# One normalisation moves from VectorE to ScalarE in each of 16 units, and the second copy of the head outputs is made by an SBUF-to-SBUF transfer

## The chip, the cores and the metric

The kernel runs on 1 core of one Trainium2 chip. The metric is the device time of one launch in microseconds (us), and the median of several runs is compared. The core has four compute engines that run their own instruction lists in order: TensorE (PE in the rows; PEld is its weight load), VectorE (DVE), ScalarE (ACT) and GpSimd (POOL). SyncE (SP) only issues transfers here. The lists meet at semaphores.

## The reference

One layer of each kind is applied to a tensor of 4 sequences, 512 tokens, 256 features: attention, feed-forward, a state-space layer, feed-forward again. The change touches the attention alone:

```python
q_c = _rms_norm(x @ wq_down.T, q_norm_w)
kv_c = _rms_norm(x @ wkv_down.T, kv_norm_w)          # 64 wide, shared by the 16 heads
...
scores = jnp.einsum('bqhd,bkhd->bhqk', q, k) * scale
scores = jnp.where(causal[None, None], scores, -jnp.inf)
probs = jax.nn.softmax(scores.astype(jnp.float32), axis=-1)
out = jnp.einsum('bhqk,bkhd->bqhd', probs, v)
return out.reshape(bs, seq_len, NH * D_V) @ wo.T
```

## The kernel before

**Number format.** Nearly every product is made in split precision: a float32 tile is copied out of PSUM in a rounded format (the "hi" part, ScalarE), and VectorE writes the remainder ("lo"). The compressed values are only 64 wide, so the head outputs are kept as 64 rows of hi and 64 rows of lo in PSUM.

**Tiling.** Attention works on 4 batches. A batch has 4 tiles of 128 query tokens, a tile 4 groups of 4 heads, so a batch has 16 units; unit `n` belongs to tile `n // 4`. Because of the causal mask a unit of tile t has scores of width (t + 1) x 128 and t + 1 blocks of transposed probabilities. The last tile (units 12 to 15 of a batch) is the widest: 512 columns a head.

**Order.** Each engine's order is written out by hand as a slot function (`pe_slot`, `act_slot`, `dve_slot`), called once for each slot `s`. In one slot the engines work on several units at once: scores and row maxima of unit s-2 and s-3, exponentials of s-3, normalisation of s-3 and s-4, transposes of s-4, values of s-5, projection of s-6. Batches follow each other without a gap. Some slots carry extra work for the next batch (down projection, squares, feature-major copies).

**Steps that the change touches.**

- `exp` (L872) writes unnormalised probabilities of one head and their sum; `recip` (L1217, DVE) turns the sums of two heads into reciprocals. `normalise` multiplies one head's probabilities by its reciprocal: on ScalarE at L897, on VectorE at L1232. `on_dve` (L51) says which: before the change, heads 2 and 3 of a unit of the last tile go to VectorE, all others to ScalarE.
- `p_transpose(b, n, j)` (L1609, PE, matmuls at L1619) needs all four heads of unit n. In `pe_slot` it follows `q_transpose` (L1593).
- `pt_high` (L906, ACT) and `pt_low` (L1241, DVE) copy the transposed block; `values` (L1633 and L1636, PE) multiplies it by the values.
- `out_high` (ACT) copies the finished 4 head outputs of a unit out of PSUM bank 6 twice: at L912 all 128 rows into `o_a`, at L914 the 64 hi rows again into the upper half of `o_b`. `out_low` (L1247, DVE) writes the remainder of the hi rows into the lower half of `o_b`.
- `project(b, n)` (L1639, PE, matmuls at L1646 and L1648) multiplies `o_a` and `o_b` by the output weights. It stands one slot after `out_high` of the same unit. `o_a`, `o_b` have two buffers, by `n % 2`.
- SyncE's list (L722) has, after the loads of the weights, four loads for the state-space weights (`ssm_nat`), and then the stores of the output.

Of the kernel before, what the change touches and what calls it, by code (L numbers as in the profile page):

```python
# [4 lines left out]
F32 = mybir.dt.float32  # L5
# [14 lines left out]
G = 4  # L20
# [19 lines left out]
def tile_of(n):  # L40
    return n // (HEADS // G)
# [8 lines left out]

def on_dve(n, h):  # L51

    return tile_of(n % UNITS) == TB - 1 and h >= 2


def by_dve(n, k=0):
# [6 lines left out]
def by_act(n, k=0):  # L63
    return G * n + k - by_dve(n, k)
# [16 lines left out]
def token_count(b, k):  # L81

    return 1 + 14 * b + k - 4 * (b - (k == 0)) if b else 1 + k


def free_after(e, sem, count):

    if not (isinstance(count, int) and count <= 0):
        e.wait_ge(sem, count)
# [18 lines left out]
def build(nc, x_in, wq_down, wq_up, wq_rope, q_norm_w, wkv_down, kv_norm_w, wkv_up, wk_rope, wo,  # L108
# [3 lines left out]
    with ctx:  # L112
# [121 lines left out]
        def sem(name):  # L234
            return ctx.enter_context(nc.semaphore(name))
# [29 lines left out]
        recip_s, norm_a, norm_d = sem("recip_s"), sem("norm_a"), sem("norm_d")  # L265
        pt_mm, pt_hi_s, pt_lo_s, pv_mm = sem("pt_mm"), sem("pt_hi_s"), sem("pt_lo_s"), sem("pv_mm")
        o_hi_s, o_lo_s, y_mm = sem("o_hi_s"), sem("o_lo_s"), sem("y_mm")
        x_add, f_add, s_add = sem("x_add"), sem("f_add"), sem("s_add")

        gu_mm, silu_s, hf_s, hhi_s, hlo_s, dn_mm = (  # L270
# [452 lines left out]
        def _(sp_):  # L723
# [31 lines left out]
                sp_.wait_ge(prep_act, V0 + 4 * k + 4)  # L755
                sp_.dma_start(wo_b[KR:P, hs, :].bitcast(F32), wo_a[KR:P, hs, :].bitcast(F32)).then_inc(wo_b_in, 16)

            sp_.wait_ge(tok, token_count(BATCH, 0))
            sp_.wait_ge(at_mm, 1 + 3 * BATCH)
            sp_.dma_start(ssm_nat[:, 0, :, :], w_in.rearrange("(c p) d -> p c d", p=P)).then_inc(ssm_in, 16)  # L760
            sp_.dma_start(ssm_nat[:, 2, :, :], w_out.rearrange("(c p) d -> p c d", p=P)).then_inc(ssm_in, 16)
            hpc = P // (DIM // 32)
            for c in range(CK):
                sp_.dma_start(ssm_nat[:, 1, c, :],
                              w_dt[c * hpc:(c + 1) * hpc, :].unsqueeze(1).to_broadcast([hpc, DIM // 32, DIM]))\
                    .then_inc(ssm_in, 16)
            for b in range(BATCH):
                for t in range(TB):
                    sp_.wait_ge(f_add, BATCH * TB + b * TB + t + 1)
# [51 lines left out]
        def _(act):  # L821
# [87 lines left out]
            def out_high(b, n):  # L909
                act.wait_ge(pv_mm, b * BLOCKS + blocks_before(n + 1))  # L910
                free_after(act, y_mm, b * UNITS + n - 1)
                nc.scalar.copy(o_a[:, n % 2, :, :].rearrange("p h d -> p (h d)"), bank[6][:, :])\  # L912
                    .then_inc(o_hi_s, 1)
                nc.scalar.copy(o_b[0:KR, n % 2, :, :].rearrange("p h d -> p (h d)"), bank[6][0:KR, :])\  # L914
                    .then_inc(o_hi_s, 1)


# [206 lines left out]
        def _(dve):  # L1124
# [92 lines left out]
            def recip(b, n, k):  # L1217

                dve.wait_ge(s_exp, 1 + b * HEADS * TB + G * n + 2 * k + 2)
                if on_dve(n - 2, 2 * k):  # L1220
                    free_after(dve, norm_d, b * by_dve(UNITS) + by_dve(n - 2, 2 * k + 2))
                else:
                    free_after(dve, norm_a, b * by_act(UNITS) + by_act(n - 2, 2 * k + 2))
                nc.vector.reciprocal(rden[:, n % 2, 2 * k:2 * k + 2], den[:, n % 2, 2 * k:2 * k + 2])\  # L1224
                    .then_inc(recip_s, 1)

# [16 lines left out]
                    .then_inc(pt_lo_s, 1)  # L1243

            def out_low(b, n):
                dve.wait_ge(o_hi_s, 2 * (b * UNITS + n) + 2)
                nc.vector.tensor_tensor(o_b[KR:P, n % 2, :, :].rearrange("p h d -> p (h d)"), bank[6][0:KR, :],  # L1247
                                        o_a[0:KR, n % 2, :, :].rearrange("p h d -> p (h d)"), ALU.subtract)\
                    .then_inc(o_lo_s, 1)
# [299 lines left out]
        def _(pe):  # L1549
# [88 lines left out]

            def project(b, n):  # L1639
                g = n % (HEADS // G)  # L1640
                pe.wait_ge(o_hi_s, 2 * (b * UNITS + n) + 2)
                pe.wait_ge(o_lo_s, 1 + b * UNITS + n + 1)
                if g == 0:
                    pe.wait_ge(x_add, 1 + b * TB + tile_of(n))
# [266 lines left out]
```

## Time and profile before

| quantity | us |
|---|---|
| median of 3 runs | 808.61 |
| lowest and highest of them | 807.47, 811.57 |
| the profiled execution | 804.74 |
| its span, first to last instruction | 802.9 |

The page of the profile gives busy time by engine, the chain of work that ended last, and groups of instructions. The attention lasts from about 30 to 551 us of the span, the other layers from there on. In the attention all four engines are busy most of the time, so a share of busy time decides little; the chain of work, read in order of time, shows which engine's work each stretch waits for. Where two records on one engine follow each other without idle time, the second starts before the first one's record ends, so the cost of an instruction in a full queue is the distance between starts and not the length of its record.

### The profile page before, as it was taken

How to read it: one execution, taken by the hardware profiler on the slowest of the kernel's cores; microseconds unless marked ns; L12 is line 12 of the kernel's file. 1: busy time of each engine (PE TensorE's matmuls, PEld its weight loads, DVE VectorE, ACT ScalarE, POOL GpSimd, SP SyncE). 2: the span in 40 equal slices, each digit the busy share in tenths (PEclk: the TensorE clock that was granted, in tenths of full speed). 3: DMA queues.
4: the chain of work that ended last, by engine and by line, in shares of the span. 5: the costliest groups of instructions: out<-in, count | busy, mean ns of one | idle time of the engine just before them, and what ended most of it. 6: DMA issues, size and time to landing. Idle time of an engine off the chain costs nothing.

```text
span 802.9 us, 15139 instructions
## 1 busy us (share of the span) xinstructions
PE 749.6 (93%) x4556; PEld 645.8 (80%) x4556; DVE 668.8 (83%) x2184; ACT 603.3 (75%) x1499; POOL 468.2 (58%) x392
## 2 busy tenths in 40 slices
PE   4889999999999999999999999989999999999998
PEld 4768788888878788888887888777888788887887
DVE  4978998998999998899998999987676878877643
ACT  3459999888999988999887899985447576674232
POOL 0579999999999999999999999950000000000000
PEclk9899999999999999999999999999999999999999
DMA  9821000000000000000001000000000000000000
GB/s 228 266 67 28 2 1 1 1 1 2 1 2 2 1 1 2 1 2 1 1 2 41 1 2 1 1 1 1 1 1 1 0 1 1 1 17 11 27 27 27
DMA packets 15536, 15.58 MB, mean 19 GB/s; under 512 B 5824, under 2 KB 14464, under 8 KB 15072
## 3 DMA queue, kind: packets, MB, share of 16 engines
q1 hardware_dynamic: 13952, 12.45, 5.5%
q0 software_dynamic: 624, 2.12, 0.8%
q8 instruction: 38, 0.62, 0.3%
q14 instruction: 42, 0.34, 0.1%
q10 hardware_dynamic: 880, 0.04, 0.1%
HBM read 11.46 MB, written 2.10 MB: 17 GB/s over the span
## 4 chain that ended last, share of the span: by engine, by line
PE 60%; ACT 14%; DVE 10%; issue 9%; DVEq 0%; ACTq 0%
PE bank L671 12%; PE bank L673 11%; PE bank L672 11%; PE bank L1619 7%; ACT prob L897 5%; ACT prob L877 3%; PE bank L1633 2%; PE bank L1636 2%; PE bank L1646 2%; DVE pt_lo L1241 2%; PE bank L1648 2%; ACT pt_hi L906 2%; PE bank L636 1%; DVE o_b L1247 1%; PE bank L1582 1%
## 5 line engine op out<-in xcount | busy, mean ns | idle before, releaser
L810 POOL TENSOR_SCALAR hot<-raw_gu,lut 128x352 f32<-128x352 int32 x120 | 177.4, 1478 | 12.2
L816 POOL TENSOR_TENSOR total<-total,hot 128x352 f32<-128x352 f32 (+1 forms) x168 | 160.3, 954 | 14.0
L877 ACT ACTIVATE prob<-bank,bias_m 128x128 f32<-128x128 f32 (+3 forms) x256 | 136.2, 532 | 19.5 <-DVE bias_m L1189 19.0
L1189 DVE CUSTOM_DVE_ANT_0 bank<-bank,mask 128x128 f32<-128x128 f32 (+3 forms) x256 | 125.7, 494 | 21.1 <-issue 19.4
L1241 DVE TENSOR_TENSOR pt_lo<-bank,pt_hi 128x512 fp32r<-128x512 f32 x160 | 109.0, 682 | 8.2 <-ACT pt_hi L906 7.3
L1619 PE MATMUL bank<-ident,prob 128*128 128x128 f32 x640 | 99.3, 278 | 17.0 <-ACT prob L897 10.0
L897 ACT ACTIVATE prob<-prob,rden 128x128 f32<-128x128 f32 (+3 forms) x224 | 110.6, 545 | 4.5 <-DVE rden L1224 3.9
L906 ACT CAST pt_hi<-bank 128x512 fp32r<-128x512 f32 x160 | 94.2, 589 | 13.2 <-PE bank L1636 7.2
L1619 PEld LDWEIGHTS bank<-ident,prob 128*128 128x128 f32 x640 | 72.9, 140 | 35.5 <-ACT prob L897 19.3
L810 POOL TENSOR_SCALAR hot<-raw_dn,lut 128x352 f32<-128x352 int32 (+1 forms) x60 | 87.6, 1459 | 6.1
L671 PE MATMUL bank<-kt_hi,qt_hi 128*128 128x128 f32 (+3 forms) x256 | 87.2, 341 | 1.8 <-ACT prob L877 1.3
L673 PE MATMUL bank<-kt_hi,qt_lo 128*128 128x128 f32 (+3 forms) x256 | 82.6, 322 | 0.0
L672 PE MATMUL bank<-kt_lo,qt_hi 128*128 128x128 f32 (+3 forms) x256 | 82.5, 322 | 0.0
L671 PE MATMUL bank<-xt_hi,gu_hi 128*128 128x512 f32 (+1 forms) x176 | 70.1, 399 | 1.6 <-DVE h_f L1391 1.6
L1633 PE MATMUL bank<-pt_hi,v_hl 128*128 128x512 f32 x160 | 68.1, 426 | 2.6 <-issue 2.4
L673 PE MATMUL bank<-xt_hi,gu_lo 128*128 128x512 f32 (+1 forms) x176 | 69.4, 394 | 0.0
L672 PE MATMUL bank<-xt_lo,gu_hi 128*128 128x512 f32 (+1 forms) x176 | 69.3, 394 | 0.0
L1646 PE MATMUL bank<-wo_a,o_a 128*128 128x256 f32 x256 | 67.9, 298 | 0.1
L992 ACT ACTIVATE silu<-bank 128x512 f32<-128x512 f32 x40 | 23.9, 597 | 56.7 <-PE bank L673 56.7
L1648 PE MATMUL bank<-wo_b,o_b 128*128 128x256 f32 x256 | 63.7, 282 | 0.0
L1636 PE MATMUL bank<-pt_lo,v_hl 128*128 128x512 f32 x160 | 63.3, 396 | 0.3 <-DVE pt_lo L1241 0.2
L671 PEld LDWEIGHTS bank<-kt_hi,qt_hi 128*128 128x128 f32 x256 | 48.5, 189 | 11.8 <-issue 2.4
(214 smaller groups left out, 2084.0 us busy)
## 6 DMA issues: line engine op xcount, KB each, us to landing
x<-in_L_attn_a_x_dram SPq DMA_DIRECT2D x4, 512.0 KB, 7.8
wo_nat<-in_L_attn_a_wo_dram SPq DMA_DIRECT2D x1, 2048.0 KB, 14.6
out_dram<-x SPq DMA_DIRECT2D x16, 128.0 KB, 1.8
wqu<-in_L_attn_a_wq_up_dram SPq DMA_DIRECT2D x2, 768.0 KB, 8.5
wo_b<-wo_a SPq DMA_DIRECT2D x2, 512.0 KB, 4.3
wqr<-in_L_attn_a_wq_rope_dram SPq DMA_DIRECT2D x4, 192.0 KB, 7.0
raw_dn<-in_L_ffn_down_idx_dram POOLq DMA_DIRECT2D x1, 688.0 KB, 7.8
raw_gu<-in_L_ffn_gate_idx_dram POOLq DMA_DIRECT2D x1, 640.0 KB, 5.2
```

What stands on the lines that cost most here:

```text
L671: nc.tensor.matmul(o, l_hi, r_hi, start=start and k == 0, stop=False)
L672: nc.tensor.matmul(o, l_hi, r_lo, start=False, stop=False)
L673: last = nc.tensor.matmul(o, l_lo, r_hi, start=False, stop=stop and k == n - 1)
L810: nc.gpsimd.tensor_scalar((hot if v else total)[:, 0:n], raw[:, c:c + n], float(v), lut[:, v:v + 1], ALU.is_equal, ALU.mult).then_inc(lut_ ...
L816: nc.gpsimd.tensor_tensor(dst, total[:, 0:n], hot[:, 0:n], ALU.add).then_inc(lut_sum, 1)
L877: nc.scalar.activation(prob[:, n % 2, h, 0:w], bank[2 + h % 2][:, 0:w], ACT.Exp, bias=bias_m[:, n % 2, h:h + 1], scale=-1.0, accum_out=den ...
L897: nc.scalar.activation(prob[:, n % 2, h, 0:w], prob[:, n % 2, h, 0:w], ACT.Copy, scale=rden[:, n % 2, h:h + 1]).then_inc(norm_a, 1)
L906: nc.scalar.copy(pt_hi[:, c % 2, :, :].rearrange("p h d -> p (h d)"), bank[4 + c % 2][:, :])\
L1189: nc.vector.tensor_tensor_reduce(out=bank[2 + h % 2][:, 0:w], in0=bank[2 + h % 2][:, 0:w], in1=mask[:, TB * P - w:TB * P], scale=1.0, scal ...
L1241: nc.vector.tensor_tensor(pt_lo[:, c % 2, :, :].rearrange("p h d -> p (h d)"), bank[4 + c % 2][:, :], pt_hi[:, c % 2, :, :].rearrange("p h ...
L1619: last = nc.tensor.transpose(bank[4 + c % 2][:, h * P:(h + 1) * P], prob[:, n % 2, h, j * P:(j + 1) * P], ident[:, :])
L1633: nc.tensor.matmul(bank[6][:, :], v, pt_hi[:, c % 2, :, :].rearrange("p h d -> p (h d)"), start=j == 0, stop=False)
```

## The change

In the last tile VectorE normalises head 3 alone, and ScalarE heads 0, 1 and 2. ScalarE's second copy in `out_high` is gone; SyncE waits for the first copy of each unit and issues a transfer of its upper 64 rows, 128 KB, from `o_a` to `o_b`, which raises one of two new semaphores, `o_dup`. `project` waits for it as well. `out_low` waits for one copy instead of two. The four `ssm_nat` loads move in SyncE's list behind the transfer of the first unit of the last batch, 49 transfers in. `recip` waits for ScalarE's normalisation of two units before in all cases, and for VectorE's where head 3 is among them.

```diff
 def on_dve(n, h):
-    return tile_of(n % UNITS) == TB - 1 and h >= 2
+    return tile_of(n % UNITS) == TB - 1 and h == G - 1
...
+            def duplicate(b, n):
+
+                sp_.wait_ge(o_hi_s, b * UNITS + n + 1)
+                sp_.dma_start(o_b[0:KR, n % 2, :, :].bitcast(F32), o_a[0:KR, n % 2, :, :].bitcast(F32)).then_inc(o_dup[n % 2], 16)
+
+            for b in range(BATCH):
+                for n in range(UNITS):
+                    duplicate(b, n)
+                    if b == BATCH - 1 and n == 0:
+                        load_ssm()
...
                 nc.scalar.copy(o_a[:, n % 2, :, :].rearrange("p h d -> p (h d)"), bank[6][:, :])\
                     .then_inc(o_hi_s, 1)
-                nc.scalar.copy(o_b[0:KR, n % 2, :, :].rearrange("p h d -> p (h d)"), bank[6][0:KR, :])\
-                    .then_inc(o_hi_s, 1)
...
-                if on_dve(n - 2, 2 * k):
+                free_after(dve, norm_a, b * by_act(UNITS) + by_act(n - 2, 2 * k + 2))
+                if on_dve(n - 2, 2 * k + 1):
                     free_after(dve, norm_d, b * by_dve(UNITS) + by_dve(n - 2, 2 * k + 2))
-                else:
-                    free_after(dve, norm_a, b * by_act(UNITS) + by_act(n - 2, 2 * k + 2))
...
-                dve.wait_ge(o_hi_s, 2 * (b * UNITS + n) + 2)
+                dve.wait_ge(o_hi_s, b * UNITS + n + 1)
...
-                pe.wait_ge(o_hi_s, 2 * (b * UNITS + n) + 2)
+                pe.wait_ge(o_hi_s, b * UNITS + n + 1)
+                pe.wait_ge(o_dup[n % 2], 16 * ((b * UNITS + n) // 2 + 1))
```

ScalarE, two slots of the last tile in the second batch, before. L897 is a normalisation, L877 an exponential, L912 and L914 the two copies of head outputs:

```order
426 L912 CAST o_a<-bank 128x512
427 L914 CAST o_b<-bank 64x512
428 L877 ACTIVATE prob,den<-bank,bias_m 128x512
429 L906 CAST pt_hi<-bank 128x512
430 L877 ACTIVATE prob,den<-bank,bias_m 128x512
431 L884 COPY q_tok<-bank 128x4x64
432 L897 ACTIVATE prob<-prob,rden 128x512 x2
433 L906 CAST pt_hi<-bank 128x512
434 L877 ACTIVATE prob,den<-bank,bias_m 128x512
435 L906 CAST pt_hi<-bank 128x512
```

and the same stretch of the changed kernel, whose lines are 13 higher on this engine (L925 is the copy, L910 the normalisation):

```order
404 L925 CAST o_a<-bank 128x512
405 L890 ACTIVATE prob,den<-bank,bias_m 128x512
406 L919 CAST pt_hi<-bank 128x512
407 L890 ACTIVATE prob,den<-bank,bias_m 128x512
408 L897 COPY q_tok<-bank 128x4x64
409 L910 ACTIVATE prob<-prob,rden 128x512 x2
410 L919 CAST pt_hi<-bank 128x512
411 L910 ACTIVATE prob<-prob,rden 128x512
412 L890 ACTIVATE prob,den<-bank,bias_m 128x512
413 L919 CAST pt_hi<-bank 128x512
```

The copy into `o_b` has gone behind L925, and the third normalisation stands behind the copy of a transposed block and ahead of the next unit's first exponential.

VectorE at the same place, before, with what each instruction waits for:

```order
785 L1189 ISA bias_m 128x1
786 L1232 TENSOR_SCALAR prob<-prob,rden 128x512 [waits recip_s] x2
787 L1241 TENSOR_TENSOR pt_lo<-bank,pt_hi 128x512 [waits pv_mm,pt_hi_s]
788 L530 MEMSET scratch 128x1 [waits s_exp,s_mm]
789 L1189 ISA bank,bias_m<-bank,mask 128x512
```

and of the changed kernel:

```order
785 L1200 ISA bias_m 128x1
786 L1242 TENSOR_SCALAR prob<-prob,rden 128x512 [waits recip_s]
787 L1251 TENSOR_TENSOR pt_lo<-bank,pt_hi 128x512 [waits pv_mm,pt_hi_s]
788 L531 MEMSET scratch 128x1 [waits s_exp,s_mm]
789 L1200 ISA bank,bias_m<-bank,mask 128x512
```

One of the two normalisations ahead of the remainder copy is gone; the rest stands as it stood.

## Rows read from the trace of the kernel before

**Rows 1.** The page: busy time, its share of the span, and instructions by engine

```profile
PE 749.6 (93%) x4556; PEld 645.8 (80%) x4556; DVE 668.8 (83%) x2184; ACT 603.3 (75%) x1499; POOL 468.2 (58%) x392
```

**Rows 2.** Windows of the second batch: start:end, length, then busy us of each engine

```profile
205.00:232.00 27.00, 25.58 (x169) 22.15 (x169) 25.84 (x106) 26.70 (x84) 25.05 (x22) 1.00 0.01 2
...
262.00:297.00 35.00, 33.72 (x198) 28.18 (x197) 33.94 (x100) 30.61 (x70) 32.60 (x27) 1.00 0.00 1
```

**Rows 3.** Chain that ended last, in time: start, us, what; all around head-output copies

```profile
69.33 0.45 ACT o_b L914
...
212.72 0.45 ACT o_b L914
213.17 0.37 ACT squares L856 x2
...
542.70 0.48 ACT o_b L914
```

**Rows 4.** The same chain around one transposition of tile 2, and of the last tile

```profile
245.41 0.24 PE bank L1636
...
246.22 1.13 ACT prob L897 x2
...
247.39 0.66 PE bank L1619 x4
...
290.15 0.24 PE bank L1636
...
290.55 0.69 DVE pt_lo L1241
...
291.37 0.63 PE bank L1619 x4
...
514.92 0.48 DVE prob L1232
```

**Rows 5.** ScalarE's instructions in order of time: start, us, line, op, tiles

```profile
258.13 0.60 ACT L914 CAST o_b<-bank 64x512 fp32r<-64x512 f32 x1
258.61 0.60 ACT L877 ACTIVATE prob<-bank,bias_m 128x384 f32<-128x384 f32 x1
...
269.80 1.35 ACT L897 ACTIVATE prob<-prob,rden 128x512 f32<-128x512 f32 x2
271.04 0.59 ACT L906 CAST pt_hi<-bank 128x512 fp32r<-128x512 f32 x1
...
280.54 0.71 ACT L877 ACTIVATE prob<-bank,bias_m 128x512 f32<-128x512 f32 x1
```

**Rows 6.** VectorE's pairs of normalisations in three slots of the last tile

```profile
271.09 1.69 DVE L1232 TENSOR_SCALAR prob<-prob,rden 128x512 f32<-128x512 f32 x2
...
280.07 0.89 DVE L1232 TENSOR_SCALAR prob<-prob,rden 128x512 f32<-128x512 f32 x2
```

**Rows 7.** TensorE between the query transposes and the transposes of probabilities, two slots

```profile
271.88 0.60 PE L1593 MATMUL bank<-ident,q_tok 128*128 128x128 f32 x4
272.88 0.63 PE L1619 MATMUL bank<-ident,prob 128*128 128x128 f32 x4 [0.41 <-issue]
...
281.75 0.60 PE L1619 MATMUL bank<-ident,prob 128*128 128x128 f32 x4
```

**Rows 8.** Last units: ScalarE's first copy, and the first matmul of the projection

```profile
542.11 0.59 ACT L912 CAST o_a<-bank 128x512 fp32r<-128x512 f32 x1
547.78 0.58 ACT L912 CAST o_a<-bank 128x512 fp32r<-128x512 f32 x1 [1.32 <-PE bank L1636]
...
547.58 0.28 PE L1646 MATMUL bank<-wo_a,o_a 128*128 128x256 f32 x1
...
549.71 0.36 PE L1646 MATMUL bank<-wo_a,o_a 128*128 128x256 f32 x1
```

**Rows 9.** Transfers, from the page: count, KB each, median us from issue to landing

```profile
out_dram<-x SPq DMA_DIRECT2D x16, 128.0 KB, 1.8
...
wo_b<-wo_a SPq DMA_DIRECT2D x2, 512.0 KB, 4.3
```

More of the change, by code:

```diff
@@ L267, in build @@
         o_hi_s, o_lo_s, y_mm = sem("o_hi_s"), sem("o_lo_s"), sem("y_mm")
+        o_dup = [sem(f"o_dup{k}") for k in range(2)]
         x_add, f_add, s_add = sem("x_add"), sem("f_add"), sem("s_add")
@@ L756, in _, with load_ssm @@
                 sp_.dma_start(wo_b[KR:P, hs, :].bitcast(F32), wo_a[KR:P, hs, :].bitcast(F32)).then_inc(wo_b_in, 16)
[L758 to L766, printed above, removed]
+            def load_ssm():
+                sp_.wait_ge(tok, token_count(BATCH, 0))
+                sp_.wait_ge(at_mm, 1 + 3 * BATCH)
+                sp_.dma_start(ssm_nat[:, 0, :, :], w_in.rearrange("(c p) d -> p c d", p=P)).then_inc(ssm_in, 16)
+                sp_.dma_start(ssm_nat[:, 2, :, :], w_out.rearrange("(c p) d -> p c d", p=P)).then_inc(ssm_in, 16)
+                hpc = P // (DIM // 32)
+                for c in range(CK):
+                    sp_.dma_start(ssm_nat[:, 1, c, :],
+                                  w_dt[c * hpc:(c + 1) * hpc, :].unsqueeze(1).to_broadcast([hpc, DIM // 32, DIM]))\
+                        .then_inc(ssm_in, 16)
+            def duplicate(b, n):
[6 more added lines that the diff above has]
+                        load_ssm()
             for b in range(BATCH):
```

## The prediction, made before the changed kernel ran

> **What bounds the kernel now.** I read the totals first: TensorE is busy for 93% of the span, VectorE 83%, ScalarE 75% [rows 1]. That says the four lists are close together, not which one a given slot waits for. So I went to the windows of one attention batch [rows 2]. In a stretch of tiles 1 and 2 (205 to 232 us) ScalarE is busy 26.70 of 27.00 us, more than TensorE's 25.58. In the last tile (262 to 297) ScalarE falls to 30.61 of 35.00, and TensorE (33.72) and VectorE (33.94) are the full ones. The change takes work from ScalarE in every unit and gives it some in the last tile, which is where it has room.
>
> Busy time is still only a rate. What an edit can gain is read in the chain of work that ended last, since taking work off it shortens the program by that much at most, and work beside it gives nothing. The second copy L914 stands on that chain 15 times out of 64 (first at 69.33, last at 542.70 us), once with 0.00 us and otherwise with about 0.45 to 0.58 us each, 6.6 us in all [rows 3]. Where it does, the piece behind it is ScalarE's too (213.17, the squares): ScalarE runs without a gap and everybody waits for it. The other 49 are elsewhere. In tile 2 the chain is TensorE back to back, then two normalisations (246.22, 1.13 us), then the transposes at 247.39; the copy had been done before [rows 4]. In the last tile it goes from the values at 290.15 over the remainder copy on VectorE (290.55, 0.69 us) to the transposes at 291.37, a loop between TensorE and VectorE that holds neither the copy nor a normalisation [rows 4].
>
> **The second copy, removed.** In a full queue it costs the distance between starts: from 258.13 to 258.61, 0.48 us, not the 0.60 of its record [rows 5]. The 64 of them are 30.7 us of ScalarE's time, and the 49 off the chain are worth nothing by it. On the chain 6.6 us is the ceiling. Another path can stand close behind, and then less comes back: I take 6.0 us and keep 3.3 (half) and 6.6 as ends. I choose near the ceiling because in these slots TensorE has room of its own: its busy time in the window is 1.42 us short of 27.00, and busy time counts the overlap of pipelined matmuls, so the true room is larger. One of the 15 also releases `out_low`, which now starts after the first copy; that is the entry at 542.70 and is in the sum.
>
> **One normalisation of two, taken from VectorE (16 units).** A pair takes 0.89 us in one unit and 1.69 us in another [rows 6], so a single one costs VectorE 0.4 to 0.9 us. Mostly that frees nothing, by the loop above: the remainder copy behind the pair waits for TensorE anyway. The exception is the first unit of each last tile. There the query transposes start at 271.88 and the transposes of probabilities at 272.88, 1.00 us later [rows 7], while another slot of the same tile has the second group directly behind the first; the pair, at 271.09 with 1.69 us, ends at 272.78 and sets the start. Only in the last batch has the printed chain such a piece (514.92, 0.48 us [rows 4]). I take 0.4 us in each of 4 batches, 1.6 us; the ends are 0 (ScalarE's third normalisation is then what TensorE waits for) and 3.6 (0.9 us each).
>
> **The third normalisation, added on ScalarE.** It costs the distance between starts, half of 271.04 minus 269.80, 0.62 us, so 9.9 us over 16 units [rows 5]. Against the 0.48 us given back in the same slot ScalarE is 0.14 us longer in a slot where it has over 1 us idle (4.39 us of 35.00 in four slots [rows 2]), so its rate costs nothing. Its place could: TensorE waits for it before the transposes. In the slot at 280 us it would start where the exponential starts now (280.54) and end 0.73 us later (1.35 for two, less the 0.62 between their starts), at 281.3; the transposes start at 281.75 [rows 5, 7]. It is hidden with 0.45 us to spare. Queued behind it are the next exponential, a copy of a transposed block and the query copy, each later by 0.62 us; ScalarE's idle time takes that up. In the tail, after the last unit's queries, there is nothing to overlap and TensorE waits closely for each copy: 0.3 us there, bounded by 0 and 0.62.
>
> **The transfer.** Two rows bracket 128 KB inside SBUF: the stores, as large, land after 1.8 us, and the 512 KB transfer between the same two kinds of memory after 4.3 us [rows 9]. I take 2.5 us, nearer the row of equal size with something for SyncE's wake-up. The copy of the last unit but one starts at 542.11 and ends at 542.70; its projection starts at 547.58 [rows 8], 4.9 us later, and all earlier units have more, since `project` stands a slot behind. Even 4.3 us fits. Only the last unit is short: its copy ends at 548.36 and the projection starts at 549.71, 1.35 us later [rows 8]. At 2.5 us it starts 1.15 us late; but some of the present start is `out_low`'s, which comes earlier, and some slack is in the weight tasks on either side, so I take 0.8 us, and keep 0.45 (1.8 us) and 2.95 (4.3 us) as ends. SyncE's own list is no obstacle: it has nothing else to do in these stretches but the four state-space loads, which now go two slots later and are wanted only after the attention. TensorE gets one more wait per unit, on an instruction that already carries two.
>
> The Trainium skill, "DMA: Bandwidth & Descriptors", section "Anatomy of one DMA — SWDGE (gpsimd) path", gives about 2.0 us fixed plus the bytes at 436 GB/s, an estimate of 2.3 us for 128 KB (that section is on transfers issued from GpSimd; these are SyncE's). The store's 1.8 us is below it, so the page does not quite agree. By it the last projection would be 0.95 us late ahead of the same allowance of 0.35, so 0.6 instead of 0.8, and the sum -6.7 instead of -6.5.
>
> **The sum**, against the profiled execution's 804.74 us: minus 6.0, minus 1.6, plus 0.3, plus 0.8, or minus 6.5, gives 798.2. The profiled execution is 3.87 us below the median of the runs, 808.61; the difference carries over and the forecast is 808.6 - 6.5 = **802.1 us**. From the ends the change is between -9.8 (6.6 and 3.6 gained, 0.45 lost) and +0.3 (3.3 gained, 2.95 and 0.62 lost), or 798.8 to 808.9.
>
> **Rivals.** (A) *ScalarE's rate counts, not the chain.* If the saturated slots are all paced by ScalarE, each gives 0.48 us whether or not the printed chain passes through its copy: 8 of 16 slots in a batch, 32 in all, 15.4 us, with the other terms -15.9 and 792.7 us. For it speaks 26.70 of 27.00 us; against it, that at 245 us, just behind that window, the chain is on TensorE already. (B) *The relief is absorbed.* Another path is close behind in each slot: only a third of the 6.6 us comes back, and VectorE's nothing; 2.2 - 1.1 gives 1.1 us, 807.5 us. For it speaks that all engines are over 90% busy in these windows. (C) *The third normalisation becomes the late one.* It stands at the head of ScalarE's slot and TensorE needs it at once. The point from which it decides is ScalarE reaching that place over 0.45 us later than now, relative to TensorE. Then each of the 16 transposes is late by up to 0.62 us plus the copy of a block ahead of it (0.48), 17.6 us at most; at half of that, 8.8, with 3.3 gained from the copies and 0.8 for the tail, the kernel is 6.3 us slower, 814.9 us. The Trainium skill, "Perfetto Trace Analysis", section "Optimizing Scalar/DVE Operations", speaks on that side: where VectorE has a fast mode for an operation it is the quicker engine, and a move to ScalarE pays only where VectorE is full. The trace agrees that the operation is dearer here (0.62 against about 0.45 us), and that VectorE is the fuller one in that window. A transfer over 4.9 us would be a further loss, but the longer row, of four times the bytes, is below that.
>
> **How the numbers follow.** The forecast 0.55, A 0.12, B 0.23, C 0.10. What a measurement of this kernel can tell from no change is about 0.5%, 4.0 us, so faster means below 804.6 and slower above 812.6. The forecast's case is below 804.6 in about nine of ten (its range reaches to 808.9), A always, B seldom (0.02), C never: 0.62 faster. C is above 812.6 in half of its cases: 0.05 slower. The rest, 0.33, is within 0.5%. For 8 in 10 the range runs from 796 to 810: it leaves out most of A (about 0.10) and the worse part of C (about 0.07). The forecast's own range is 798.8 to 808.9.
>
> **What would show it.** If the steps are right, ScalarE's total falls by about 38 us of records for the copies and rises by about 12 for the normalisations; the stretch corresponding to 205 to 232 us gets shorter by 1 to 1.5 us; 262 to 297 by about half a us; the transfers take 2 to 3 us and TensorE never waits for them except once, near the end of the attention; the rest of the program is as long as before. The prediction is wrong if TensorE waits for L910, the normalisation, in the last tile (C), if each slot of tiles 1 and 2 is shorter by 0.4 us or more (A), or if ScalarE shows new idle time in those slots while their length stays (B).

## The result, and the profile after

Eight runs, the profiled one among them, gave the changed kernel a median of 804.52 us (800.97 to 806.35). Eight runs of the kernel before gave 807.74 us (805.85 to 811.57). The ratio is 0.9956, 95% interval [0.9937, 0.9975]. That is 3.2 us less, where 6.5 were forecast. The time lies inside the range. By the bound of 0.5% that the prediction set it counts as no change, if only just (0.44%), but the interval leaves out 1: the change works, at half the size.

Here is the page of the changed kernel: busy time, the clock in 40 slices, the chain that ended last by engine, and the group of the exponentials (busy us, mean ns, then ScalarE's idle time before them and what ended it).

```profile
PE 752.3 (94%) x4556; PEld 648.2 (81%) x4556; DVE 661.9 (82%) x2168; ACT 587.4 (73%) x1451; POOL 467.6 (58%) x392
...
PEclk9599999999999999999999999999999999999999
...
PE 60%; issue 12%; DVE 12%; ACT 9%; DVEq 0%; ACTq 0%
...
L890 ACT ACTIVATE prob<-bank,bias_m 128x128 f32<-128x128 f32 (+3 forms) x256 | 135.6, 530 | 31.6 <-DVE bias_m L1200 30.6
```

and three of these of the kernel before:

```profile
PEclk9899999999999999999999999999999999999999
...
PE 60%; ACT 14%; DVE 10%; issue 9%; DVEq 0%; ACTq 0%
...
L877 ACT ACTIVATE prob<-bank,bias_m 128x128 f32<-128x128 f32 (+3 forms) x256 | 136.2, 532 | 19.5 <-DVE bias_m L1189 19.0
```

ScalarE's busy time fell by 15.9 us against [rows 1]; its share of the chain fell from 14% to 9%, and the shares of VectorE and of "issue" rose. These shares move between executions: a second trace of each kernel, taken later, has 55% TensorE, 16% ScalarE, 11% VectorE before, and 56%, 9%, 15% changed. ScalarE's fall is clear of that, TensorE's 60% is not a fixed number. The exponentials, which VectorE's row maxima (`bias_m`) release, waited 19.0 us for them before and 30.6 us now. So the copy did go, and ScalarE waits more.

On the chain the copies now look like this (start, us, what). It passes through L925, the only copy left, once in 64 units; it passes through VectorE's remainder L1257 21 times (16 before). The second traces agree: 18 copies L914 with 7.9 us and 16 remainders before, no copy and 26 remainders changed.

```profile
73.07 0.49 ACT o_a L925
...
203.70 0.57 DVE o_b L1257
...
210.20 0.64 DVE o_b L1257
```

**A measure that doesn't depend on the start.** The changed kernel's profiled execution took 806.35 us and spanned 804.6, longer than the 802.9 of the kernel before, although it is the faster kernel. The reason stands ahead of the attention's steady part. The clock row shows a piece of it: the granted clock of the second slice (20 to 40 us), behind a first slice in which TensorE was 0.4 busy, is 5 tenths, the level of 1.2 GHz, where the kernel before has 8 tenths, a mixture of both levels; the means over the span are 0.985 and 0.994. The clock is not all of it, though: the second execution of the kernel before has 8 tenths in that slice too, and begins its steady part as late as the changed kernel. These are TensorE's first matmuls of the queries of the third unit (the last number in brackets, where there is one, is idle time before), before and after:

```profile
45.12 0.48 PE L1582 MATMUL bank<-wa_hi,qa_hi 128*128 128x512 f32 x1
```

```profile
49.59 0.49 PE L1592 MATMUL bank<-wa_hi,qa_hi 128*128 128x512 f32 x1
```

They start 4.5 us apart, and a second execution of the unchanged kernel has this matmul at 49.34. Over all kernels that follow it lies between 45.1 and 49.6 us, in no order that goes with the edits. What sets the start is open. So I compare in every trace two stretches: from this matmul to the first matmul of the last projection, which holds nearly all that the change touches, and from there to the end of TensorE's last matmul. Each stretch is read from one execution. Each ratio is against the runs of the kernel before beside it (medians 806.87 to 807.74) and need not be the quotient of the printed medians.

| kernel | steady stretch, us | behind it, us | median, us | ratio to before, 95% |
|---|---|---|---|---|
| before | 504.59 | 250.39 | 807.74 | |
| before, again | 504.66 | 250.31 | (one run) | |
| changed | 501.73 | 250.38 | 804.52 | 0.9956 [0.9937, 0.9975] |
| changed, again | 501.02 | 251.79 | 804.14 | 0.9958 [0.9939, 0.9977] |
| transfer alone | 503.81 | 250.31 | 806.20 | 0.9994 [0.9977, 1.0011] |
| normalisation alone | 501.70 | 251.69 | 804.36 | 0.9957 [0.9939, 0.9975] |
| alternating heads, no last transfer | 500.38 | 250.37 | 803.18 | 0.9960 [0.9935, 0.9986] |
| changed, no last transfer | 499.85 | 250.36 | 803.46 | 0.9955 [0.9938, 0.9971] |
| before, light remainder | 500.14 | 250.44 | 800.29 | 0.9928 [0.9905, 0.9951] |
| transfer alone, light remainder | 495.58 | 250.39 | 797.98 | 0.9900 [0.9858, 0.9942] |
| changed, light remainder | 493.81 | 250.39 | 798.79 | 0.9898 [0.9869, 0.9927] |
| before, two small copies more | 511.23 | 250.34 | 815.17 | 1.0108 [1.0083, 1.0133] |

The two traces of the kernel before agree within 0.07 us over 504, those of the changed kernel within 0.7. The mean of the latter, 501.4, is 3.2 us below the former, as the medians say. Behind it the changed kernel has 250.38 us in one execution and 251.79 in the other, so the 1.4 us there go with the execution and not with an edit.

### The profile page after: what moved, and what is told of

It is laid out like the page before. It is cut to its first block, busy times and chain, and to the rows that moved or that the text cites. A ratio compares the mean times of both kernels' runs of the same rounds, so it can differ in the third digit from the quotient of the medians.

```text
span 804.6 us, 15155 instructions
## 1 busy us (share of the span) xinstructions
PE 752.3 (94%) x4556; PEld 648.2 (81%) x4556; DVE 661.9 (82%) x2168; ACT 587.4 (73%) x1451; POOL 467.6 (58%) x392
## 3 DMA queue, kind: packets, MB, share of 16 engines
q0 software_dynamic: 624, 2.12, 0.9%
## 4 chain that ended last, share of the span: by engine, by line
PE 60%; issue 12%; DVE 12%; ACT 9%; DVEq 0%; ACTq 0%
PE bank L672 12%; PE bank L674 11%; PE bank L673 11%; PE bank L1629 7%; ACT prob L910 5%; PE bank L1646 2%; PE bank L1643 2%; PE bank L1657 2%; PE bank L1659 2%; DVE pt_lo L1251 2%; DVE o_b L1257 2%; ACT prob L890 1%; ACT pt_hi L919 1%; DVE bias_m L1200 1%; PE bank L1592 1%
## 5 line engine op out<-in xcount | busy, mean ns | idle before, releaser
L890 ACT ACTIVATE prob<-bank,bias_m 128x128 f32<-128x128 f32 (+3 forms) x256 | 135.6, 530 | 31.6 <-DVE bias_m L1200 30.6
L910 ACT ACTIVATE prob<-prob,rden 128x128 f32<-128x128 f32 (+3 forms) x240 | 122.2, 553 | 6.5 <-DVE rden L1234 5.0
L1251 DVE TENSOR_TENSOR pt_lo<-bank,pt_hi 128x512 fp32r<-128x512 f32 x160 | 109.1, 682 | 12.7 <-ACT pt_hi L919 12.2
```

The costliest lines, as they stand in the source:

```text
L890: nc.scalar.activation(prob[:, n % 2, h, 0:w], bank[2 + h % 2][:, 0:w], ACT.Exp, bias=bias_m[:, n % 2, h:h + 1], scale=-1.0, accum_out=den ...
L910: nc.scalar.activation(prob[:, n % 2, h, 0:w], prob[:, n % 2, h, 0:w], ACT.Copy, scale=rden[:, n % 2, h:h + 1]).then_inc(norm_a, 1)
L1251: nc.vector.tensor_tensor(pt_lo[:, c % 2, :, :].rearrange("p h d -> p (h d)"), bank[4 + c % 2][:, :], pt_hi[:, c % 2, :, :].rearrange("p h ...
```

## The experiments

**The changed kernel again**, beside the three that follow, as their common measure.

> The changed kernel once more, next to its parts on the same chip. The recorded profile of it had a TensorE clock of 0.78 in its first 36 us, and its first unit's queries came 2.54 us later than before, 4.47 us later two units on; from there to the last unit it gained 2.6 us. Expected if that start was a matter of the one execution: a profile whose first units come at the times of the kernel before within 0.5 us, the same slot lengths in the attention within 0.1 us, and a ratio to before of 0.994 to 0.998. If the transfers had something to do with the late start, it is late by 3 to 5 us again.

Measured: 804.14 us against 807.16, ratio 0.9958. The first result stands. The start came neither with the kernel before nor 3 to 5 us later: the third unit's queries begin at 47.55 us, 2.4 us later. The slots repeat to 0.1 us with few exceptions, the largest two slots of the first batch that differ by 0.5 us and cancel.

**The transfer alone.** Heads 2 and 3 go back to VectorE; the transfer stays.

```diff
 def on_dve(n, h):
-    return tile_of(n % UNITS) == TB - 1 and h == G - 1
+    return tile_of(n % UNITS) == TB - 1 and h >= 2
```

> Only the second copy is replaced by the transfer; VectorE normalises heads 2 and 3 of the last tile as before. Theory T1 (VectorE's list is tied with ScalarE's in tiles 1 and 2, so that ScalarE's relief turns into waiting for row maxima): the attention is shorter by 0 to 1.5 us, the tail 1 us longer, total 0 to -1 us; the changes of +0.2, -0.5, +0.5 us in the slots of the last tile are absent. Theory T2 (the relief of ScalarE gave the gain, as the chain of work had it, and the third normalisation cost some of it): -4 to -6 us.

Measured: 0.9994 [0.9977, 1.0011], and the steady stretch is 0.8 us shorter than before. The last transfer costs 0.98 us of that (shown below), so 64 copies, 30.7 us of ScalarE's time and 6.6 us of the chain, gave 1.8 us. With 0.7 us between two traces of one kernel this is a rough number, but it is far from T2's 4 to 6. On the chain the remainder L1257 now stands 24 times with 14.4 us, where it had 16 times and 10.1 us.

Why shows in one slot of tile 1 of the second batch. First ScalarE before (start, us, line, tiles; idle time in brackets), between the squares and the query copy:

```profile
207.18 0.46 ACT L877 ACTIVATE prob<-bank,bias_m 128x256 f32<-128x256 f32 x1
...
207.62 0.46 ACT L877 ACTIVATE prob<-bank,bias_m 128x256 f32<-128x256 f32 x1
```

and the same place with the transfer alone, and under it VectorE there:

```profile
206.14 0.46 ACT L890 ACTIVATE prob<-bank,bias_m 128x256 f32<-128x256 f32 x1
...
206.88 0.47 ACT L890 ACTIVATE prob<-bank,bias_m 128x256 f32<-128x256 f32 x1 [0.20 <-DVE bias_m L1200]
```

```profile
205.76 0.68 DVE L1251 TENSOR_TENSOR pt_lo<-bank,pt_hi 128x512 fp32r<-128x512 f32 x1
206.37 0.42 DVE L1200 CUSTOM_DVE_ANT_0 bank<-bank,mask 128x256 f32<-128x256 f32 x1
...
206.71 0.13 DVE L1200 DVE_READ_ACCUMULATOR2_ANT bias_m<- 128x1 f32 x1
206.88 0.68 DVE L1257 TENSOR_TENSOR o_b<-bank,o_a 64x512 fp32r<-64x512 f32 x1
```

The two exponentials started 0.44 us apart before and start 0.74 us apart now: ScalarE has lost the copy ahead of them and stands still until VectorE, with no gap between the records shown, has written the row maximum. The slot, from 204.92 to 211.33 us before, is 6.41 us long, and with the transfer alone 6.43. The next slot is 0.55 us shorter, and the one behind it 0.53 longer. From unit 5 (192.98 us before) to unit 11 (232.67) the removals add up to less than 0.1 us. The 1.8 us are 0.7 in tile 1 of the first batch, 0.6 at the end of the last tile in the first two batches, and 0.5 ahead of the last projection.

**The normalisation alone.** The kernel before, with head 3 alone on VectorE and the waits that belong to it.

```diff
 def on_dve(n, h):
-    return tile_of(n % UNITS) == TB - 1 and h >= 2
+    return tile_of(n % UNITS) == TB - 1 and h == G - 1
```

> Only the split of the normalisations changes; ScalarE makes both copies as before. T1: -2 to -3 us, made in the first unit (about 0.7 us a batch) and the third (0.5) of each last tile and partly lost again in the second (0.2) and fourth (0.5); slots of tiles 0 to 2 as before. T2: no gain or a loss of 1 to 3 us, since ScalarE then has 1.10 us more in those slots than the changed kernel's copy relief pays for.

Measured: 0.9957 [0.9939, 0.9975], the steady stretch 2.9 us shorter. This half is the whole gain by the medians. With the 0.8 us of the other half it makes 3.7, the 3.2 of both together within the spread of the traces.

Where it comes from, in the changed kernel. In the first slot of the last tile, where the pair took 1.69 us [rows 6] and the transposes of probabilities came 1.00 us behind those of the queries [rows 7], VectorE and then TensorE read:

```profile
273.98 1.00 DVE L1242 TENSOR_SCALAR prob<-prob,rden 128x512 f32<-128x512 f32 x1
274.90 0.68 DVE L1251 TENSOR_TENSOR pt_lo<-bank,pt_hi 128x512 fp32r<-128x512 f32 x1
```

```profile
274.77 0.60 PE L1603 MATMUL bank<-ident,q_tok 128*128 128x128 f32 x4
275.21 0.64 PE L1629 MATMUL bank<-ident,prob 128*128 128x128 f32 x4
```

The distance is 0.44 us, so 0.56 of the 1.00 is gone, and the slot is 0.69 us shorter. That one was forecast. The next was not: the slot around 290 us, whose chain in [rows 4] I had read as a loop between TensorE and VectorE with no normalisation in it. Before, on VectorE and TensorE:

```profile
289.05 1.58 DVE L1232 TENSOR_SCALAR prob<-prob,rden 128x512 f32<-128x512 f32 x2
290.55 0.68 DVE L1241 TENSOR_TENSOR pt_lo<-bank,pt_hi 128x512 fp32r<-128x512 f32 x1
```

```profile
288.39 0.39 PE L1636 MATMUL bank<-pt_lo,v_hl 128*128 128x512 f32 x1
...
289.99 0.39 PE L1636 MATMUL bank<-pt_lo,v_hl 128*128 128x512 f32 x1
290.22 0.60 PE L1593 MATMUL bank<-ident,q_tok 128*128 128x128 f32 x4
291.37 0.63 PE L1619 MATMUL bank<-ident,prob 128*128 128x128 f32 x4 [0.55 <-DVE pt_lo L1241]
```

and the same place of the changed kernel:

```profile
291.58 0.67 DVE L1242 TENSOR_SCALAR prob<-prob,rden 128x512 f32<-128x512 f32 x1
292.17 0.67 DVE L1251 TENSOR_TENSOR pt_lo<-bank,pt_hi 128x512 fp32r<-128x512 f32 x1
```

```profile
292.52 0.39 PE L1646 MATMUL bank<-pt_lo,v_hl 128*128 128x512 f32 x1
292.75 0.60 PE L1603 MATMUL bank<-ident,q_tok 128*128 128x128 f32 x4
293.19 0.60 PE L1629 MATMUL bank<-ident,prob 128*128 128x128 f32 x4
```

The pair ended at 290.63 us and the remainder copy's record began at 290.55: it followed directly. The chain puts its start down to TensorE's matmul at 289.99, but the kernel does not make it wait for that one. It waits for ScalarE's copy of its own block and, since there are two buffers, for the values of the block two before (`c` is the block's number in its batch):

```python
dve.wait_ge(pt_hi_s, b * BLOCKS + c + 1)
free_after(dve, pv_mm, b * BLOCKS + c - 1)
```

The copy, ScalarE's at 288.93 us, had ended at 289.52, and the matmul two blocks before, at 288.39, at 288.78. Both were done a full microsecond earlier. The changed kernel shows the same: its remainder copy starts at 292.17, ahead of the matmul at 292.52 that stands where the one at 289.99 stood. So the pair alone held the copy. The chain infers a releaser from the semaphore event that came last, and that event was of a later block than the one waited for. With one normalisation gone VectorE is early, and TensorE's wait of 0.55 us is gone too.

Not all of it stays. In the slot behind it, ScalarE's third normalisation pushes the copy of a transposed block. In the changed kernel, on ScalarE, VectorE and TensorE:

```profile
301.09 0.74 ACT L910 ACTIVATE prob<-prob,rden 128x512 f32<-128x512 f32 x1
...
302.06 0.60 ACT L919 CAST pt_hi<-bank 128x512 fp32r<-128x512 f32 x1
```

```profile
302.69 0.69 DVE L1251 TENSOR_TENSOR pt_lo<-bank,pt_hi 128x512 fp32r<-128x512 f32 x1 [0.47 <-ACT pt_hi L919]
...
303.82 0.28 DVE L1217 TENSOR_TENSOR q_rot<-bank,sin 128x128 f32<-128x128 f32 x1
```

```profile
304.25 0.48 PE L1592 MATMUL bank<-wa_hi,qa_hi 128*128 128x512 f32 x1 [0.28 <-DVE q_rot L1217]
```

Before, this last matmul, at 301.75 us, waited for nothing. The balance of each slot, as the change in the distance between the first query matmuls of neighbouring units (us, against before), is given below. In the five last rows the changes repeat from batch to batch within about 0.2 us, but for the last unit's slot with the transfer alone (-0.47, -0.24 and 0.00).

| slot that starts with, in the second batch | before | changed | normalisation alone | transfer alone |
|---|---|---|---|---|
| tile 2, first unit (211.33) | 6.89 | -0.55 | -0.03 | -0.55 |
| its second unit (218.22) | 6.90 | +0.43 | +0.01 | +0.53 |
| last unit of the last tile (265.92) | 8.91 | -0.69 | -0.63 | -0.23 |
| next batch, unit 0 (274.83) | 8.98 | +0.25 | +0.09 | 0.00 |
| unit 1 (283.81) | 9.64 | -0.48 | -0.49 | +0.03 |
| unit 2 (293.45) | 8.30 | +0.53 | +0.54 | +0.04 |
| unit 4 (309.69) | 7.06 | -0.31 | -0.28 | +0.12 |

Here the normalisation moves only the slots that process the last tile, the transfer mostly others. In other batches slots elsewhere shift too, by up to 1 us, and mostly shift back in the next ones; one of them, unit 5 of the last batch, is about 1 us shorter than in the first trace of before in every other kernel, and 0.43 us shorter in the second trace of before. Both lose again what they gained within a slot or two, but the normalisation keeps about 0.7 us a batch.

**Alternating heads, and no last transfer.** VectorE keeps heads 2 and 3 in odd units, and head 3 in even ones; the last unit of the program has its second copy on ScalarE.

```diff
 def on_dve(n, h):
-    return tile_of(n % UNITS) == TB - 1 and h == G - 1
+    return tile_of(n % UNITS) == TB - 1 and h >= G - 1 - n % 2
...
-                for n in range(UNITS):
+                for n in range(UNITS - (b == BATCH - 1)):
...
+                if b == BATCH - 1 and n == UNITS - 1:
+                    nc.scalar.copy(o_b[0:KR, n % 2, :, :].rearrange("p h d -> p (h d)"), bank[6][0:KR, :])\
+                        .then_inc(o_hi_s, 1)
```

> The changed kernel with two edits: in the last tile VectorE normalises heads 2 and 3 of the odd units (13 and 15 of each batch) and head 3 of the even ones, and the last unit of all has its second copy made by ScalarE again. By T1 and the slot lengths: the losses of 0.2 us (unit 13) and 0.5 us (unit 15) go away, 0.7 us a batch or 2.8 us, and the tail gives back 1.0 us: 3 to 4 us faster than the changed kernel, 6 to 7 us faster than before. If the losses in units 13 and 15 come from somewhere else than the third normalisation, only the 1 us of the tail shows.

Measured: 0.9960 [0.9935, 0.9986]; the steady stretch is 1.0 us shorter than the changed kernel's, 500.4 against 501.4. That is the tail alone; the next kernel, without the alternation, is even 0.5 us shorter. The alternation took the loss of 0.53 us in the slot of unit 2 away (+0.09), so the third normalisation was its cause. It lost what unit 4 had gained (from -0.31 to +0.12), and the smaller loss of unit 0, which should have gone as well, stayed (from +0.25 to +0.37). These balance, and the 3 to 4 us that I expected did not come.

**The changed kernel without the last transfer alone.** The second and third piece of that diff, with their waits.

> The changed kernel, but the last unit's second copy is made by ScalarE again, so that the last projection waits for no transfer. Both theories: the distance between the last two projections goes from 3.1 back to 2.1 us, 0.98 us off the changed kernel's time, with nothing else changed: 803.2 to 803.5 us beside 804.5. If SyncE's transfer was not what the last projection waits for, the distance stays at 3.1 us.

Here are the last two projections (first matmul each) and ScalarE's last copy, of the changed kernel and then of the one without the last transfer. They answer to [rows 8]. The third fence has the changed kernel's 64 transfers: the issue in ns (min/median/max), first and last start, and the time to landing.

```profile
548.41 0.59 ACT L925 CAST o_a<-bank 128x512 fp32r<-128x512 f32 x1 [1.31 <-PE bank L1646]
```

```profile
548.21 0.28 PE L1657 MATMUL bank<-wo_a,o_a 128*128 128x256 f32 x1
...
551.32 0.36 PE L1657 MATMUL bank<-wo_a,o_a 128*128 128x256 f32 x1 [1.12 <-issue]
```

```profile
L773 SPq DMA_DIRECT2D o_b<-o_a x64: 461/462/507, 73.6 to 549.0; - x64
...
DMA to landing us min/median/max: 2.2/2.2/2.7
```

```profile
545.34 0.28 PE L1663 MATMUL bank<-wo_a,o_a 128*128 128x256 f32 x1
...
547.46 0.36 PE L1663 MATMUL bank<-wo_a,o_a 128*128 128x256 f32 x1
```

```profile
546.02 0.58 ACT L928 CAST o_b<-bank 64x512 fp32r<-64x512 f32 x1
```

The distance is 3.11 us with the transfer and 2.12 without, as before (549.71 less 547.58 [rows 8] is 2.13). The last transfer was issued at 549.0 and lands 2.2 us later, at 551.2, and the matmul starts at 551.32. It is the only one of the 64 projections whose first matmul has idle time before it. The term is 0.98 us. In the median, 803.46 us, it can't be told from the changed kernel's 804.14 to 804.52, nor are the ratios apart (0.9955 and 0.9956 to 0.9958): these medians don't resolve 1 us. The steady stretch is 1.5 us below the mean of the changed kernel's two, the 0.98 and 0.5 more that lie within their spread.

**Is VectorE the path behind?** This is the test of the main reading. The remainder of the head outputs, L1247, is written for 32 of 512 columns from the third unit on, which takes about 0.5 us a unit from VectorE and leaves older values in the other columns. It is done to the kernel before, to the one with the transfer alone, and to the changed one.

```diff
-                nc.vector.tensor_tensor(o_b[KR:P, n % 2, :, :].rearrange("p h d -> p (h d)"), bank[6][0:KR, :],
-                                        o_a[0:KR, n % 2, :, :].rearrange("p h d -> p (h d)"), ALU.subtract)\
+                w = G * P if b == 0 and n < 2 else 32
+                nc.vector.tensor_tensor(o_b[KR:P, n % 2, :, :].rearrange("p h d -> p (h d)")[:, 0:w], bank[6][0:KR, 0:w],
+                                        o_a[0:KR, n % 2, :, :].rearrange("p h d -> p (h d)")[:, 0:w], ALU.subtract)\
```

The kernel before, again, as their measure:

> The kernel before, profiled once more. In the four profiles of changed kernels the lengths of the attention's slots repeat to 0.02 us, but the first units begin 0.4 to 3.7 us (in the first profile of the changed kernel 4.5) later than in the one profile of before, and the feed-forward part is 0 or 1.4 us longer. Expected if that is chance of the execution: this profile differs from the first one of before in the same two places and nowhere else, with the slots from unit 2 on the same to 0.05 us. If it is the edits, this profile repeats the first.

Measured: 808.94 us in one run, the steady stretch 504.66. Its start is 4.22 us later and the part behind is the same. The slots do not all repeat to 0.05 us: some of the first batch differ by 0.1 to 0.2, two neighbours of the last by +0.35 and -0.43, and the sum is the same to 0.1 us.

> The kernel before with a lighter VectorE: from the third unit on, the remainder copy into the lower half of the second operand (L1247, 0.69 us) writes 32 of 512 columns. The lower half of that operand is stale there, so the output is not the reference's. T1 (two lists tied: VectorE's and ScalarE's): little gain, 0 to 5 us, because ScalarE's list holds the slots of tiles 1 and 2 when VectorE's gives way. If VectorE's list alone paces these slots: 0.4 to 0.6 us in each of 7 or 8 slots a batch, 12 to 18 us.

> The transfer in place of ScalarE's second copy (as in dup_only), and the lighter VectorE of before_light, with the same part left out. T1: with VectorE light the removed copy pays what the chain of work had promised, 0.3 to 0.5 us in each saturated slot: dup_light is faster than before_light by 5 to 10 us, where dup_only was faster than before by about 1. If the printed chain was wrong about ScalarE altogether, or VectorE alone paces, the two light kernels differ by the same 1 us or so.

Measured: 0.9928 for the lighter VectorE alone, 0.9900 with ScalarE's copy gone as well. In the steady stretch, which resolves more:

| | full remainder | light remainder | what the light one gives |
|---|---|---|---|
| second copy by ScalarE | 504.6 | 500.1 | 4.5 |
| second copy by the transfer | 503.8 | 495.6 | 8.2 |
| what the transfer gives | 0.8 | 4.6 | |

The same removal of the same copies is worth 0.8 us beside the full VectorE list and 4.6 beside the light one (1.8 and 5.5 without the cost of the last transfer). The difference of 3.8 us between the two is well above the 0.7 us by which two traces of one kernel differ, though each light kernel has one trace. Their medians differ by 2.3 us, with intervals that overlap, and 4.6 is a little under the 5 to 10 that were expected. The 4.5 us of the light remainder by itself lie in the range for tied lists (0 to 5), far from the 12 to 18 of a VectorE that paces alone.

The ceiling was not reached: in the kernel with the light remainder the copy L914 stands on the chain 19 times with 8.8 us (in the two traces of before 15 and 18 times, 6.6 and 7.9 us), and 5.5 came back. The chain by engine, for the transfer alone, the light remainder alone, and both:

```profile
PE 59%; DVE 14%; issue 12%; ACT 8%; DVEq 0%; ACTq 0%
```

```profile
PE 60%; ACT 18%; issue 8%; DVE 7%; DVEq 0%; ACTq 0%
```

```profile
PE 66%; ACT 10%; issue 9%; DVE 8%; DVEq 0%; ACTq 0%
```

Take ScalarE's copy away and the chain leans to VectorE (14%, against 10 and 11% in the traces of before); lighten VectorE and it leans to ScalarE (18%, against 14 and 16%); do both and TensorE has 66%, against 60 and 55%. The first two steps are small beside the spread, the third is not. With both edits the remainder stands on the chain 7 times with 1.8 us, where the transfer alone left 24 times and 14.4.

Two limits. The total wait of the exponentials for row maxima does not tell whether the copy pays: it is 33.1 us with the transfer alone and 33.4 us with the light remainder beside it, where the copy did pay. And the edit lightens the very instruction that had taken over on the chain, one that TensorE's next values wait for as well. So VectorE's path is shown to be the one behind; whether it is the load of its whole list or this one instruction in its place, no run separates.

**The changed kernel with the light remainder.** Is the normalisation's gain VectorE's relief as well?

> The changed kernel with the remainder of the head outputs written for 32 of 512 columns from the third unit on (the other columns keep older values, so the output isn't the reference's), the same edit as in the two light kernels before. If VectorE's relief is what the moved normalisation gives (T1), then with a lighter VectorE list less of it is left: the attention from the queries of unit 2 to the last projection is at most 1.5 us shorter than with the transfer and the light list alone (495.6 us), or not shorter, plus about 1 us behind it for the last transfer. If the normalisation's gain is independent of how full VectorE is, the stretch is 2 to 3 us shorter, about 493 us.

Measured: the steady stretch is 1.8 us below that of the transfer alone with the light remainder (493.8 and 495.6). Beside the full remainder the same step is worth 2.4 (503.8 less 501.4). That lies between the two expectations (at most 1.5, and 2 to 3), and the traces do not resolve which is nearer. The medians, 798.79 and 797.98 us, show no gain at all, within their intervals. How much of the normalisation's gain depends on VectorE's load is open.

**More work on ScalarE.** Two copies of 64x64 from bank 6 into an unused tile, each unit, on the kernel before.

```diff
+                free_after(act, spare_s, 2 * (b * UNITS + n))
+                for j in range(2):
+                    nc.scalar.copy(spare[0:KR, 64 * j:64 * j + 64], bank[6][0:KR, 0:64]).then_inc(spare_s, 1)
```

> The kernel before with a longer ScalarE list: two more copies of 64x64 per unit out of the same bank into an unused tile, about 0.35 to 0.4 us of ScalarE time a unit. T1 and the chain alike: ScalarE is on the chain in tiles 1 and 2, so the whole of it shows in about 7 slots of 16 in each batch, 9 to 12 us slower. If ScalarE had room in those slots (its relief was worthless because nobody waited for it), less than 3 us slower.

Measured: 1.0108 [1.0083, 1.0133], the steady stretch 6.6 us longer. The pair on ScalarE, and the copy behind it:

```profile
211.51 0.33 ACT L918 CAST spare<-bank 64x64 fp32r<-64x64 f32 x2
211.71 0.61 ACT L919 CAST o_b<-bank 64x512 fp32r<-64x512 f32 x1
```

It holds ScalarE for 0.20 us from start to start, half of what was expected, 12.8 us in 64 units, and half of that reached the end. The 6.6 us lie between the two expectations (9 to 12, and under 3); at 0.20 us in 7 slots of 16 the first would have been 5.6. They are not spread evenly, though: in two batches the slot of tile 2's second unit alone is 1.2 us longer, which is more than was added there, and why is open. So in one direction 12.8 us of ScalarE cost 6.6, in the other 30.7 us gave 1.8. That fits two lists that are tied: more work on one counts nearly in full where it is full, less work on it counts only until the other holds.

## Why the forecast was right in sign and wrong in size

**The second copy: -6.0 forecast, -1.8 measured.** This is the main step that failed. The place was right (15 of 64 copies on the chain) and 6.6 us held as a ceiling, and I took nearly all of it "because in these slots TensorE has room of its own". That asked one other engine and forgot the nearer one: VectorE was busy 25.84 of 27.00 us in the same window, more than TensorE [rows 2], and ScalarE's exponentials wait for its row maxima. Even the lower end, 3.3, was too high. The stretch between 204.92 and 232.67 us, which should have been 1 to 1.5 us shorter, is exactly as long (27.75 us) in the changed kernel. That VectorE's path took the relief is shown by the 2 x 2 table: with its remainder lighter, the same copies are worth 5.5.

**VectorE's normalisation and ScalarE's third: -1.6 and +0.3 forecast, -2.9 measured for the two.** The mechanism was right for the first slot of each last tile, and the size too small: it gave 0.6 to 0.8 in the kernel with the normalisation alone, not 0.4. A second step failed, "the remainder copy behind the pair waits for TensorE anyway". It waited for the pair alone, as the counts in the kernel show, so one more slot of each batch gained 0.5 us. About 0.5 us a batch was then lost to the third normalisation. In the tail the third normalisation cost nothing that shows: from the last unit's queries to the last projection the kernel with the normalisation alone is 0.7 us shorter than before (40.73 and 41.39 us), not 0.3 longer.

**The last transfer: +0.8 forecast, +0.98 measured**, from a landing time of 2.5 taken and 2.2 measured. From the start of the copy L925 at 548.41 to the matmul it is 2.91 us, against 1.93 before: the record of the copy, 0.59, the 2.2, and 0.12 from landing to matmul. With 2.2 in its place my sum would have been 0.85 less the allowance of 0.35 for slack, 0.5, so that allowance was not there. By the Trainium skill, "DMA: Bandwidth & Descriptors", section "Anatomy of one DMA — SWDGE (gpsimd) path", the estimate was 2.3 us; the trace has 2.2, so it came nearer than my choice, though the section speaks of another queue.

**The sum.** -1.8, -2.9 and +0.98 give -3.7; the two halves together give -3.2, and the half microsecond between them is within the spread. The copy was booked 4.2 us too high and the normalisations 1.6 us too low, so that the total missed by less than its largest term; that is luck. That the time lies inside the range owes to the range, which reached past no change. The starting value, a median of three runs, was 0.9 us above the median of eight. The profile of before lies 3.87 us below it because of its start: its second execution took 4.20 us more (808.94), and the third unit's queries started 4.22 us later.

**The rivals.** (B) had the right mechanism for the copy, "a third comes back" (1.8 of 6.6 and not the 2.2 it named), and its sign is there: more idle time on ScalarE at the same length of slots. Its other half, that VectorE's relief gives nothing, was wrong. I gave it 0.23; for the copy it deserved more. (A), that ScalarE's rate paces all slots, is refuted: 15.4 us were expected and 4.6 (5.5 without the cost of the last transfer) are the most that any kernel shows. (C) was present in small: the third normalisation did become the late one, once a batch, not for the transposes but for the copy of a block behind it, for 0.5 us and not for 0.62 in each unit.

**What was to be seen.** ScalarE's records lost 38.0 us of L914 and the normalisations grew from 110.6 to 122.2, as written. The busy total fell by 15.9 only, since overlapping records count once in it. The slots from 265.92 to 293.45 us are 0.9 us shorter, where about half a us was expected of 262 to 297. What stays open is why tile 1 of the first batch keeps 0.7 us of what the copy gives there, and the other batches give all of it back.

## What to carry to other kernels

The time that an instruction has on the chain that ended last is what its removal can give at most, and two executions of one kernel gave 6.6 and 7.9 us for it here. Before it is booked, find the engine that comes second in that very slot, whose list it is that releases the next instruction, and count that engine's gaps. If two paths are both full there, relieving one gives little and relieving both gives more than the sum of the two (0.8 us for one, 4.5 for the other, 9.0 for both here). Where the chain names a releaser, read in the kernel which count the instruction waits for: a semaphore that rises just before the start may have passed that count long ago, and then it is the instruction ahead on the same engine that sets the start.

## What the runs showed of the hardware

- The start of the program varied by 4.2 us between two executions of the same kernel (the same matmul at 45.12 and at 49.34 us), while the 500 us that follow repeated within 0.1 to 0.7 us. A difference of 3 us is better read there than in the medians.
- A transfer of 128 KB from SBUF to SBUF, 64 rows of 2 KB, issued by SyncE, landed after 2.2 us in the median (2.7 at most), and its issue took 0.46 us of SyncE's queue. Beside 64 of them ScalarE's copy L925 has a mean of 606 ns against 609 before, and VectorE's L1251 has 682 ns against 682.
- VectorE's single 128x512 normalisation took from 0.48 to 1.19 us by its record in the 16 units of the changed kernel, as the pairs took 0.89 to 1.69 [rows 6]. GpSimd is busy 32.60 of 35.00 us there [rows 2]. The Trainium skill, "SBUF — State Buffer", section "Who interferes with whom", says that this operation in its fast mode and GpSimd shut each other out for a whole instruction. The spread of the records would fit; no run here took GpSimd's work away, so it isn't shown.
